# Ternary weights, signs and masks made in pieces inside the first attention's steps of a four-layer Trainium2 kernel

## What is computed

```
x = x + tanh(g_xattn[0]) * L0_xattn(ctx, ctx, layernorm(x))   # 16 heads, exp features, softmax over 77 keys
x = x + tanh(g_ffn[0])   * (layernorm(x) @ sign(W_ffn0).T)
x = x + tanh(g_xattn[1]) * L1_xattn(layernorm(x), ctx, ctx)   # one head
x = x + tanh(g_ffn[1])   * bitlinear(gelu(bitlinear(layernorm(x), W1, b1)), W2, b2)
x = ... L2_xattn (mask, 64 of 77 keys kept), L2_ffn (8 experts), L3_xattn, L3_ffn

def bitlinear(x, W, b):
    w_scale = clip(mean(abs(W)), 1e-5)
    Wq = clip(round(W / w_scale), -1, 1) * w_scale            # ternary weights
    x_scale = clip(max(abs(x), axis=-1), 1e-5)
    xq = clip(round(x * 127 / x_scale), -128, 127) * x_scale / 127
    return xq @ Wq.T + b
```

## Time and profile before

| | |
|---|---|
| median of 3 runs | 894.8 us |
| span of the profiled execution, first to last instruction | 892.7 us |
| the profiled execution's own time | shown as its span alone |
| busy: TensorE, VectorE, ScalarE, POOL | 793.7, 655.2, 491.1, 542.3 us |
| share of TensorE in the chain that ended last | 58% |
| share of VectorE in it | 23% |
| DMA in the first fortieth of the span | 284 GB/s |

### The profile page before, as it was taken

How to read it: one execution, slowest core, us unless ns; L and a number is a source line. 1 busy time by engine, 2 the same in 40 slices (tenths; PEclk the granted TensorE clock), 3 DMA queues, 4 the chain that set the end, 5 groups by cost and what they waited for, 6 DMA issues and landing times.

```text
span 892.7 us, 18849 instructions
## 1 busy us (share of the span) xinstructions
PE 793.7 (89%) x5796; PEld 623.2 (70%) x5802; DVE 655.2 (73%) x2739; ACT 491.1 (55%) x1280; POOL 542.3 (61%) x729
## 2 busy tenths in 40 slices
PE   7999998998788666867877979999999999998897
PEld 5677776886566444645655869788878879887775
DVE  4888776889979999999999863465555542526887
ACT  5777764568886897979887231222212112226673
POOL 3565643687863978888776126455555655237883
PEclk9999999999999697989999999999999999999999
DMA  8200001000000082000123622222222243140011
GB/s 284 75 1 2 1 2 48 1 1 1 1 2 1 1 336 89 1 26 7 66 72 119 196 72 43 31 43 43 36 43 42 37 99 46 19 108 1 13 36 48
DMA packets 37822, 46.70 MB, mean 52 GB/s; under 512 B 4326, under 2 KB 33870, under 8 KB 37723
## 3 DMA queue, kind: packets, MB, share of 16 engines
q1 hardware_dynamic: 29243, 35.77, 11.9%
q0 software_dynamic: 8480, 9.72, 7.1%
HBM read 33.80 MB, written 11.68 MB: 51 GB/s over the span
## 4 chain that ended last, share of the span: by engine, by line
PE 58%; DVE 23%; POOL 6%; issue 5%; ACT 5%; DMA 1%; another core or an unknown queue 1%; DVEq 0%; SPq 0%; POOLq 0%; ACTq 0%
PE ps L3018 10%; PE ps L3029 10%; DVE experts L1818 4%; PE ps L2460 3%; DVE experts L1804 3%; PE ps L2487 3%; PE ps L2364 3%; PE ps L3073 2%; PE ps L3047 2%; DVE m L1797 2%; DVE m8b L1811 2%; PE ps L2445 2%; PE ps L2472 2%; PE ps L2806 2%; PE ps L2786 1%
## 5 line engine op out<-in xcount | busy, mean ns | idle before, releaser
L2086 DVE COPY ptall<-experts 128x512 f32 x136 | 53.7, 437 | 98.0 <-PE ps L3018 51.9
L1394 ACT ACTIVATE wk<-ps 128x1024 f32<-128x1024 f32 x34 | 34.8, 1025 | 146.4 <-PE ps L3018 81.2
L3018 PE MATMUL ps<-xnT,ptall 128*128 128x128 f32 x896 | 105.0, 275 | 2.3 <-DVE ptall L2086 1.8
L3018 PEld LDWEIGHTS ps<-xnT,ptall 128*128 128x128 f32 x896 | 102.4, 192 | 3.1 <-issue 2.2
L3029 PE MATMUL ps<-experts,wk 128*128 x448 | 102.0, 381 | 1.4 <-ACT xkeep L1404 1.4
L3029 PEld LDWEIGHTS ps<-experts,wk 128*128 128x128 f32 x448 | 82.9, 190 | 17.0 <-issue 6.8
L855 POOL DMA_INDIRECT xn<-expert_in,rown x34 | 36.7, 1081 | 80.3 <-PE ps L3004 53.2
L879 POOL DMA_INDIRECT token_sum<-xkeep,dest x28 | 48.5, 1733 | 31.5 <-ACT xkeep L1404 24.5
L646 POOL TENSOR_TENSOR experts<-experts,rden 128x616 f32<-128x616 f32 x32 | 38.9, 1217 | 46.8 <-DVE rden L1578 46.8
L1236 ACT ACTIVATE experts<-experts 128x77 f32<-128x77 f32 x248 | 62.2, 259 | 0.0
L762 POOL TENSOR_TENSOR experts<-experts,mx 128x616 f32<-128x616 f32 x31 | 38.0, 1226 | 33.3 <-DVE experts L1818 33.1
(11 more groups left out here) (385 smaller groups left out, 2360.3 us busy)
## 6 DMA issues: line engine op xcount, KB each, us to landing
experts<-in_ew SPq DMA_DIRECT2D x16, 1024.0 KB, 7.8
xkeep<-in_bw SPq DMA_DIRECT2D x2, 1024.0 KB, 7.8
expert_in<-xkeep SPq DMA_DIRECT2D x8, 256.0 KB, 3.4
x<-token_sum SPq DMA_DIRECT2D x8, 256.0 KB, 3.9
out<-x SPq DMA_DIRECT2D x7, 256.0 KB, 2.4
x<-in_x SPq DMA_DIRECT2D x1, 1536.0 KB, 9.6
token_sum<-x SPq DMA_DIRECT2D x4, 256.0 KB, 2.6
token_sum<-x SPq DMA_DIRECT2D x1, 1024.0 KB, 4.5
```

What stands on the lines that cost most here:

```text
L2086: ins = nc.vector.tensor_copy(tilew[:, v, c, :], experts[:, bass.ds(e * EW + (c * FF + v * 512), 512)])
L3018: ins = nc.tensor.matmul(ps[j % 2][:, v, k * P:(k + 1) * P], tilew[:, v, c, k * P:(k + 1) * P], xTb[j % 3][:, c, :], start=c == 0, stop=c ...
```

## The change

`stage2` gets its own place in a free part of `experts`, and SP issues the load of W2 right behind that of W1, with no wait. The VectorE preparations are cut into pieces and put inside the steps of the first attention: `prepare(k, slot)` is called in step k at four places, 0 (behind total 0 of the batch), 1 (behind total 1), 2 (behind total 2) and 3 (the end of the step). A ternary weight is made in four pieces of 512 columns, the comparison going straight to the ternary weight's place and combined there. The sums over partitions are made by one matmul ahead of the scores of i = 17 (batch 4, group 1). The two memsets of POOL move into steps 3 and 4 of the next stage.

```diff
-        stage2 = xkeep[:, 8:16, :].rearrange("p t d -> p (t d)")
+        stage2 = spare(EW)
@@ sync
+            sp.dma_start(stage2.rearrange("p (c n) -> p c n", c=FF // P),
+                         a["bw2"].rearrange("(c p) n -> p c n", p=P)).then_inc(s_bw2, 16)
...
-            if phases >= 3:
-                sp.wait_ge(f_p[0].sem, f_p[0].past(B))
-                sp.dma_start(stage2.rearrange("p (c n) -> p c n", c=FF // P),
-                             a["bw2"].rearrange("(c p) n -> p c n", p=P)).then_inc(s_bw2, 16)
@@ gpsimd, in the next stage's loop
+                    if k in (3, 4):
+                        vall_zeros(k - 3)
@@ vector
+                if i == TOTALLED:
+                    c3.step(nc.vector.tensor_reduce(wstat[:, 0:2], bank(4)[:, GK:GK + PARTS]
+                                                    .rearrange("p (k n) -> p k n", k=2), AX.X, ALU.add))
...
+            def prep_size(n):
+                if n == 0:
+                    ve.wait_ge(s_w[3], 3 * 16)
+                if n == 4:
+                    ve.wait_ge(s_bw2, 16)
+                c3.step(nc.vector.tensor_reduce(wpart[:, n:n + 1], staged(n), AX.X, ALU.add, apply_absolute_value=True))
...
+            def prep_signs(part):
+                if part == 0:
+                    ve.wait_ge(s_w[1], 2 * 16)
+                    c1.step(nc.vector.tensor_scalar(sign_tmp, sign_w, 0.0, None, ALU.is_lt))
+                else:
+                    c1.settle()
+                    c1.step(nc.vector.scalar_tensor_tensor(sign_w, sign_w, 0.0, sign_tmp, ALU.is_gt, ALU.subtract))
+                    c1.link(nc.vector.tensor_scalar(rows[:, 0, :], rows[:, 0, :], gates[0:KEYS, 1:2], None, ALU.mult))
+
+            def prep_bounds():
+                c3.settle()
+                c3.link(nc.vector.tensor_scalar(wstat[:, 2:4], wstat[:, 0:2], 1.0 / (D * FF), EPS_Q, ALU.mult, ALU.max))
+                c3.step(nc.vector.tensor_scalar(wstat[:, 4:6], wstat[:, 2:4], 0.5, None, ALU.mult))
+                c3.step(nc.vector.tensor_scalar(wstat[:, 6:8], wstat[:, 2:4], -0.5, None, ALU.mult))
+
+            def prep_ternary(n):
+                c3.settle()
+                if n < PARTS:
+                    k = n // 4
+                    c3.step(nc.vector.tensor_scalar(ternary(n), staged(n), wstat[:, 4 + k:5 + k], None, ALU.is_gt))
+                if n:
+                    k = (n - 1) // 4
+                    c3.step(nc.vector.scalar_tensor_tensor(ternary(n - 1), staged(n - 1), wstat[:, 6 + k:7 + k],
+                                                           ternary(n - 1), ALU.is_lt, ALU.subtract))
...
+            def prepare(k, slot):
+
+                if k in (4, 5):
+                    prep_size(4 * (k - 4) + slot)
+                elif k == 6 and slot < 2:
+                    prep_masks(slot)
+                elif k == 6:
+                    prep_signs(slot - 2)
+                elif k == 7 and slot == 0:
+                    prep_bounds()
+                elif k in (7, 8) or k == 9 and slot < 2:
+                    prep_ternary(4 * (k - 7) + slot - 1)
+                elif k == 9 and slot == 2:
+                    prep_factors()
...
                     lx_total(k - 3, 0)
                     if k == 3:
                         ctx_values(4)
+                    prepare(k, 0)
                     lx_soft(k - 3, 2)
                     lx_total(k - 3, 1)
                     if 3 <= k < 6:
                         ctx_values(k + 2)
+                    prepare(k, 1)
                     lx_soft(k - 3, 3)
                     lx_total(k - 3, 2)
+                    prepare(k, 2)
                     lx_total(k - 3, 3)
...
-                    if phases >= 4:
-                        top_masks()
-                    mid_ternary(0)
-                    mid_signs()
                 if 0 <= k - 4 < B:
                     lx_sum(k - 4)
+                prepare(k, 3)
...
-                    if 1 <= k < 7:
-                        mid_ternary(k)
@@ tensor
+                if i == TOTALLED:
+                    pe.wait_ge(prep_v[3].sem, prep_v[3].past(PARTS))
+                    nc.tensor.matmul(bank(4)[:, GK:GK + PARTS], ones[:, :], wpart[:, :], start=True, stop=True)
...
-                    if 0 <= k - 1 < 2:
-                        mid_total(k - 1)
```

More of the change, by code:

```diff
@@ L690, in mid_hidden, with vall_zeros @@
                                             ).then_inc(ghq, 1)
-            gp.wait_ge(pv_p[0].sem, pv_p[0].past(SC))
-            for h in range(2):
+            def vall_zeros(h):
+                gp.wait_ge(pv_p[0].sem, pv_p[0].past(SC))
                 nc.gpsimd.memset(pair2[:, :, :, h, :, 16 - 16 * h:32 - 16 * h].rearrange("p b c h e -> p (b c) h e"),
@@ L1594, in mid_signs @@
[L1594 to L1622, removed]
-                else:
[L1624 to L1627, removed]
-                        c3.step(nc.vector.tensor_scalar(vtmp, stg, wstat[:, 4 + k:5 + k], None, ALU.is_gt))
-                    else:
-                        c3.step(nc.vector.scalar_tensor_tensor(tern[:, :, :].rearrange("p c n -> p (c n)"), stg,
-                                                               wstat[:, 6 + k:7 + k], vtmp, ALU.is_lt, ALU.subtract))
[L1632 to L1636, removed]
-                    c3.link(nc.vector.tensor_tensor(wstat[:, 5:6], wstat[:, 5:6], gates[:, 5:6], ALU.mult))
-                    assert c3.n == TERN
@@ new lines, in _, with staged, ternary @@
+            sign_w = sgw[:, :, :].rearrange("p c n -> p (c n)")
+            sign_tmp = xng[0][:, :, :].rearrange("p t d -> p (t d)")
+            tern_flat = [v[:, :, :].rearrange("p c n -> p (c n)") for v in (tern1, tern2)]
+            def staged(n):
+                part = n % 4
+                return (stage1, stage2)[n // 4][:, part * PIECE:(part + 1) * PIECE]
+            def ternary(n):
+                part = n % 4
+                return tern_flat[n // 4][:, part * PIECE:(part + 1) * PIECE]
@@ new lines, in prep_size, with prep_masks @@
+            def prep_size(n):
[4 more added lines that the diff above has]
+                c3.step(nc.vector.tensor_reduce(wpart[:, n:n + 1], staged(n), AX.X, ALU.add, apply_absolute_value=True))
+            def prep_masks(part):
+                if part == 0:
+                    ve.wait_ge(s_w[4], 5 * 16)
+                    c4.link(nc.vector.tensor_scalar(cols[:, 12:14], cols[:, 5:7], -0.25, None, ALU.mult))
+                    c4.step(nc.vector.tensor_scalar(mrow, mrow8[:, :], -BIG, BIG, ALU.mult, ALU.add))
+                else:
+                    c4.step(nc.vector.tensor_scalar(w2o, w2o, gates[:, 2:3], None, ALU.mult))
+                    c4.step(nc.vector.tensor_reduce(mcol[:, :], mrow8[:, :].rearrange("p (b k) -> p b k", b=B), AX.X,
+                                                    ALU.max))
@@ new lines, in prep_factors @@
+            def prep_factors():
+                c3.step(nc.vector.tensor_scalar(b2bc, b2bc, gates[:, 5:6], None, ALU.mult))
+                c3.link(nc.vector.tensor_scalar(wstat[:, 4:6], wstat[:, 2:4], -1.0 / QB, None, ALU.mult))
+                c3.link(nc.vector.tensor_tensor(wstat[:, 5:6], wstat[:, 5:6], gates[:, 5:6], ALU.mult))
+                assert c3.n == TERN
+            def prepare(k, slot):
[11 more added lines that the diff above has]
+                    prep_factors()
@@ L2593, in mid_values2 @@
                 ins.then_inc(v2p, 1)
-            def mid_total(k):
-                pe.wait_ge(prep_v[3].sem, prep_v[3].past(k + 1))
-                nc.tensor.matmul(bank(3)[:, k:k + 1], ones[:, :], wstat[:, k:k + 1], start=True, stop=True).then_inc(tsp, 1)
             def freed(s, n):
```

22 lines of the change are left out of this document (10 added, 12 removed).

## The result

The changed kernel took 901.66 us (901.10 to 902.73) where the kernel before took 894.86 (894.63 to 895.24): a ratio of 1.0075, 95% interval 1.0059 to 1.0090, so slower by 6.8 us. Forecast were 897.9 us and a range up to 901.0. The direction was right, the loss is 2.2 times the forecast one (6.8 for 3.1 us), and the time lies outside the range.

The account below looks back on a forecast made before the run. TensorE was taken to bound the first attention, with a load and sum stall behind it. Span 892.7 + 6.2 cost - 3.1 gain = 895.8, plus 2.1 from span to median: 897.9 us, range 892.0 to 901.0.

Parts of the forecast that it names:

- What bounds the kernel: First attention: TensorE sets the time, and VectorE work is free until it makes TensorE wait.
- POOL gets in between: Attention steps 6 to 9: POOL's normalisation enters pairs, combinations end 1.0 us later; all losses together 6.2 us.
- Rivals 1 and 3: Attention pairs: (1) VectorE keeps the pair, POOL late, 892.2, chance 0.24; (3) blocked about every second time, 895.0, chance 0.12.
- the signs' scaling and the bounds: Small VectorE operations: scaling at step 6's last place, 0.29 us lost; bounds at place 0 of step 7, 0.05 lost.
- The total's matmul: Step 7 of the attention: one 128x8 matmul on TensorE, put at 0.25 us and counted in full.
- The gain behind the attention: Third sign product 2.5 us earlier, plus 0.58 us of TensorE wait in the second attention: 3.1, between 2.0 and 4.5.
- rival 2: Places 0 of steps 6 and 7: two-column bounds and wide mask meet POOL, up to 1.1 us each; 900.1, chance 0.09.

Follow-up runs that it names:

- e6_odd: The changed kernel with its three two-column operations for the bounds written as six of one column: 901.16 us, ratio 1.0055.
- e5_tail: The change with sums and masks left in the attention, signs, bounds and first weight ahead of its last sum, second weight right behind it: ratio 0.9992.
- e8_later: e5_tail with the second weight's comparison and half its combination ahead of the last sum, the other half behind the third statistics: 892.02 us, ratio 0.9967.
- e7_again: The changed kernel run once more, unchanged, as the level for other kernels: 902.65 us, ratio 1.0075 to the kernel before.
- e0_again: The changed kernel run once more, unchanged, as the level for other kernels: 901.51 us, ratio 1.0062 to the kernel before.
- e2_load: The kernel before with only the second ternary weight's load moved to its own place in the opening block: 896.02 us, ratio 1.0000.
- e3_swapped: The changed kernel with each pair turned round, combination of the piece before first, comparison second: 901.79 us, ratio 1.0060.
- e4_warm: The changed kernel with 24 added bf16 products of 128 columns in each of TensorE's two longest waits: 901.52 us, ratio 1.0059.
- e1_reduced: The changed kernel with each of the eight combinations replaced by a sum of magnitudes over the same 512 elements: 895.87 us, ratio 1.0002.
- e9_single: The changed kernel with comparisons and combinations one at a place, bounds in one column, signs and masks behind the last step: 893.25 us, ratio 0.9973.

## Why the prediction was wrong, point by point

**What bounds the kernel**: right. TensorE set the pace through step 6, and the sums and masks in steps 4 to 6 cost nothing (the scores start as in the kernel before, to 0.01 us, until the place of the total).

**POOL gets in between** (the end of 6.2 us that I took): right in mechanism and size. Step 8 was to lose 3.62 us and lost 3.61; step 9 was to lose 1.71 and lost 1.70; the combinations took 1.70 for 1.69 expected. Rivals 1 and 3 are out, since every pair at places 0 to 2 was blocked, in every execution.

**The step that failed: the signs' scaling and the bounds, put at 0.29 and 0.05 us of loss, measured at 0.88 and 1.06.** For the last place of step 6 I had 0.50 for the scaling and 0.35 for the meeting with POOL's bias; from its start to the next instruction it was 1.40. For place 0 of step 7 I had 0.31 for all three bounds; from the first of them to the next maximum it was 1.33 (85.81 to 87.14), the third alone 1.19. I had let a combination lose the whole of POOL's instruction and these short ones only a part or nothing: I applied the mechanism by the size of an instruction and not by its position. e6_odd shows it for the bounds (behind place 0 of step 7 it lost 0.17 us in place of 1.06). For the scaling it is read from the rows; e5_tail and e8_later took both signs and bounds out, and their scores were 0.1 us late. The total's matmul, a term that no row had, measured 0.12 us for my 0.25. Together this makes step 7 end 1.4 us later than forecast, and 1.4 us is what A has above the forecast (7.6 for 6.2) where no fall of the clock is added.

**The clock**: not in the prediction at all. Where VectorE set the pace a fall cost nothing; executions with a fall at the end of the crowded part, the first one among them, have an A 1.6 us longer.

**The gain behind the attention**: 2.5 us forecast for the third sign product, 2.4 measured (14.77 to 12.39), and 3.55 by the last one (53.42 to 49.87 us behind the end) where I had 3.1. The number was right, one reason of it only half: the sum was in my term as well as the load, but I read the chain's 5.43 us of load as the larger part. With the load alone 0.9 us came. What counts is how soon the third statistics follow the second.

**Rivals by time**: 900.1 (rival 2) was the nearest, 1.6 below the median. It has the failed term in it, but its 2.2 us were for the bounds and the mask, and the mask cost nothing: that its number is near is in part luck. The range ended at 901.0, as if no second loss could be added to rival 2.

**The sum again, by runs**: A 7.6 to 9.3, the gain -3.55, makes 4.1 to 5.7 of the 5.6 to 6.8 us. Between 1.1 us (first) and 2.6 us (e7_again) are left, and their cause stays open; a late start of the softmax is one candidate, and the lengths are of one execution while the medians are of several. Later parts differ too. From the first to the last product of the gated layer (L2718, L2692 before) it was 60.5 us in the kernel before, e0_again and e2_load, but 61.7 and 61.9 in the two other executions of the changed kernel, 61.7 to 62.0 in e3_swapped, e4_warm and e6_odd, and 62.1 in e5_tail, with a clock of 0.83 to 0.91 somewhere between 220 and 250 us; e1_reduced, e8_later and e9_single stand at 60.7 or 60.8 with a fall there too. Whether earlier ternary work sets this off, or chance, the runs don't tell. The selection stage took 206.0 to 206.4 us in some profiles and 207.2 to 207.5 in others, of every version, the kernel before in its shown profile at 206.4 and e2_load, its nearest relative, at 207.5: a spread between executions that hides about 1 us.

## What to carry to other kernels

When VectorE gets idle time to fill beside a busy GpSimd, put one instruction at a place, not two: right behind the reciprocal the single combination kept its own length eight times of eight (GpSimd's instruction paid 0.4 us instead), while the second of a pair paid 1.0 us of GpSimd's 1.35, even at two columns. Look where GpSimd is released by VectorE's own instruction (here the reciprocal), since that puts it exactly behind what is inserted next. And of a stall behind a load, ask what the engine does after the load has come; taking away the load alone gave 0.9 of 2.4 us. Idle time at the end of the stage was as good a place here (892.02 against 893.25 us, with overlapping intervals).

## What the runs showed of the hardware that was not expected

An instruction of VectorE over 128x2 elements took 1.19 us instead of 0.17 where GpSimd's stood waiting; over 128x1, at the same place, 0.14. The first comparison or combination of a pair was never held up at places 0 to 2 (0.43 or 0.70 us), and the second always was, by 1.0 us, in six executions with pairs. TensorE's granted clock fell to 0.53 for 3 us behind a stretch in which it was busy for 1.48 of 3 us, and stayed at 1.00 with 24 small bf16 products in the gap. Such a stretch did not always bring a fall: in e6_odd TensorE was busy for 1.39 us from 112 to 115 us, and the clock stood at 1.00 behind it.
